# A weighing and a last sum move from VectorE to ScalarE copies and GpSimd operations, and a GpSimd step waits for VectorE's gate

## The reference

```python
h = tok(x)                                   # position, nesting and segment embeddings, times W
h = h + attention(layernorm(h))              # 8 heads of 16, softmax over 512 keys, output matrix
xf = layernorm(h)
g = softmax(xf @ gate_w.T) - sigmoid(xf @ thr_w.T) / 4        # 4 experts
w = max(g, 0);  w = w / (sum(w) or 1)                         # (n, 4)
hidden = relu(einsum('ni,ehi->neh', xf, fc1_w))
lo = einsum('neh,ehr->ner', hidden, lora_A)                   # rank 16
lo = einsum('ner,ero->neo', lo, lora_B)
out = einsum('ne,ned->nd', w, einsum('neo,edo->ned', lo, fc2_w))
return h + out
```

## Time and profile before

| what | value |
|---|---|
| time, median of 3 runs | 1127.43 us (1126.55 to 1129.59) |
| the profiled execution's own time | 1126.86 us |
| span in its profile | 1125.1 us |
| PE busy | 1040.1 us, 92% |
| DVE busy | 948.8 us, 84% |
| ACT busy | 807.0 us, 72% |
| POOL busy | 682.1 us, 61% |
| chain that ended last, by engine | PE 64%, DVE 16%, DMA 6%, ACT 5% |

### The profile page before, as it was taken

One profiled execution on the slowest core, in us unless ns is written; L12 is line 12 of the kernel. 1 busy time (PEld: TensorE's weight loads), 2 busy tenths in 40 slices (PEclk: granted clock), 3 DMA queues, 4 the chain that ended last, 5 costly groups with the idle time before them and its releaser, 6 DMA issues.

```text
span 1125.1 us, 20263 instructions
## 1 busy us (share of the span) xinstructions
PE 1040.1 (92%) x6158; PEld 407.9 (36%) x6158; DVE 948.8 (84%) x2442; ACT 807.0 (72%) x1578; POOL 682.1 (61%) x684
## 2 busy tenths in 40 slices
PE   4368999999999999999999999999999999989865
PEld 2112233333434434343433443434343343333322
DVE  7498899999989989899999999999999998887312
ACT  2217787777877788787877778778787777856731
POOL 1855676677666666677666666667766666621231
PEclk9558999999999999999999999999999999999997
DMA  2553645555554445555555545565555554541111
GB/s 74 148 135 89 137 106 135 129 137 127 137 130 124 126 121 130 142 127 134 126 137 126 126 121 132 130 143 126 137 125 137 128 126 113 121 96 36 55 50 32
DMA packets 93530, 132.43 MB, mean 118 GB/s; under 512 B 18205, under 2 KB 69918, under 8 KB 87398
## 3 DMA queue, kind: packets, MB, share of 16 engines
q1 hardware_dynamic: 91872, 129.54, 47.9%
q10 hardware_dynamic: 1550, 1.59, 0.6%
HBM read 89.20 MB, written 35.01 MB: 110 GB/s over the span
## 4 chain that ended last, share of the span: by engine, by line
PE 64%; DVE 16%; DMA 6%; ACT 5%; issue 2%; POOL 1%; SPq 1%; POOLq 0%; ACTq 0%; DVEq 0%
PE pv L737 17%; PE mix L750 15%; PE sc L724 13%; DVE negmax L1025 9%; PE mix L804 7%; DMA den_dram<-ctx_sb 4%; PE mix L787 3%; DVE bn L1015 2%; ACT probs L592 2%; PE mix L809 2%; DVE h L1050 2%; PE mix L825 2%; DMA den<-den_dram 2%; ACT qk L596 1%; PE mix L769 1%
## 5 line engine op out<-in xcount | busy, mean ns | idle before, releaser
L1025 DVE TENSOR_REDUCE negmax<-mix 128x1 f32<-128x512 f32 x1024 | 649.0, 679 | 56.8 <-PE mix L750 56.2
L592 ACT ACTIVATE probs<-sc 128x512 f32<-128x512 f32 x1024 | 556.3, 600 | 118.2 <-PE sc L724 112.0
L724 PE MATMUL sc<-qstk,kstk 120*128 120x512 bf16 x1024 | 364.2, 382 | 5.6 <-ACT probs L592 4.9
L750 PE MATMUL mix<-kstk,qstk 96*128 96x512 bf16 x1024 | 331.7, 395 | 24.6 <-DMA kstk<-stack_dram 7.3
L737 PE MATMUL pv<-probs,vals 128*32 128x512 f32 x2048 | 244.8, 595 | 0.0
L528 POOL TENSOR_TENSOR ctxh<-ctx_sb,rdenb 128x512 f32<-128x512 f32 x64 | 81.0, 1268 | 245.3 <-DMA rdenb<-rden_dram 244.5
L750 PEld LDWEIGHTS mix<-kstk,qstk 96*128 96x128 bf16 x1024 | 89.4, 98 | 266.5 <-DVE negmax L1025 76.1
L724 PEld LDWEIGHTS sc<-qstk,kstk 120*128 120x128 bf16 x1024 | 100.1, 98 | 107.5 <-ACT probs L592 33.4
L804 PE MATMUL mix<-xn2T,fc1T_sb 128*128 128x512 f32 x256 | 138.2, 622 | 0.7 <-ACT hid L646 0.7
L508 POOL TENSOR_TENSOR qk<-qk,rstdb 128x512 f32<-128x512 f32 x64 | 81.1, 1269 | 57.9 <-DMA rstdb<-rstd_dram 53.4
L737 PEld LDWEIGHTS pv<-probs,vals 128*32 128x32 f32 x2048 | 59.1, 109 | 117.4 <-issue 100.1
(11 more groups left out here) (141 smaller groups left out, 1088.5 us busy)
## 6 DMA issues: line engine op xcount, KB each, us to landing
stack_dram<-pieces SPq DMA_DIRECT2D x192, 128.0 KB
rdenb<-rden_dram SPq DMA_DIRECT2D x64, 256.0 KB
qstk<-stack_dram SPq DMA_DIRECT2D x31, 384.0 KB, 6.6
kstk<-stack_dram SPq DMA_DIRECT2D x31, 384.0 KB, 8.8
rstdb<-rstd_dram SPq DMA_DIRECT2D x32, 256.0 KB, 3.4
wrow<-w_dram SPq DMA_DIRECT2D x32, 256.0 KB
out<-out_sb SPq DMA_DIRECT2D x32, 256.0 KB, 2.6
qstk<-stack_dram SPq DMA_DIRECT2D x31, 256.0 KB, 7.0
```

The source lines that it names most:

```text
L592: act.activation(probs[:, c % 8, i % 2], sc[:, i % RING], ACT.Exp).then_inc(s_exp, 1)
L724: pe.matmul(sc[:, i % RING, :], kstk[0:KROWS, u, h, j * P:(j + 1) * P], qstk[0:KROWS, u, h, :], start=True, stop=True).then_inc(s_score, 1)
L750: pe.matmul(max_bank(m), qstk[0:STK, u, h, j * P:(j + 1) * P], kstk[0:STK, u, h, :], start=True, stop=True).then_inc(s_mxmm, 1)
L1025: dve.tensor_reduce(negmax[:, m // NT, m % NT:m % NT + 1], max_bank(m), AX.X, ALU.max, negate=True).then_inc(s_max, 1)
```

## The change

`weigh` and `finish` leave VectorE's list. ScalarE gets two copies out of the `mix` banks, `low` in slot 4 ahead of `qk` and `out` in slot 7, after which the bank is free; GpSimd then multiplies and adds in place in SBUF: `weigh` behind `norm2`, `finish` behind `third` and ahead of `normalise`. TensorE's next users of the two banks wait for the copies. `normalise` of sequence b gets one more wait: until VectorE has finished the gates of sequence b-1 (both belong to one step), except for the last sequence. On SyncE the store of the output moves behind `rden_in`. `add_attention` waits until `finish` of two sequences before has read its buffer of `h2`.

```diff
 ACT_WORK = [
-    (1, 1, "relu", -3, 3), (4, 0, "qk", 3, 0), (4, 0, "qk", 3, 1), (4, 0, "ctx", -1, 1), (6, 0, "xn2T", -2, 0),
-    (8, 0, "gates", -2, 0), (9, 1, "gate_exp", -2, 0), (9, 1, "relu", -2, 0), (10, 1, "relu", -2, 1),
+    (1, 1, "relu", -3, 3), (4, 0, "low", -3, 0), (4, 0, "qk", 3, 0), (4, 0, "qk", 3, 1), (4, 0, "ctx", -1, 1), (6, 0, "xn2T", -2, 0),
+    (7, 0, "out", -3, 0), (8, 0, "gates", -2, 0), (9, 1, "gate_exp", -2, 0), (9, 1, "relu", -2, 0), (10, 1, "relu", -2, 1),
...
 DVE_WORK = [
-    (3, 1, "add_pos", 4, 0), (3, 1, "stats1", 4, 0), (3, 1, "weigh", -3, 0), (6, 0, "stats1", 4, 1),
-    (6, 1, "moments1", 4, 0), (7, 1, "finish", -3, 0), (7, 1, "invert_den", -1, 0),
+    (3, 1, "add_pos", 4, 0), (3, 1, "stats1", 4, 0), (6, 0, "stats1", 4, 1),
+    (6, 1, "moments1", 4, 0), (7, 1, "invert_den", -1, 0),
...
 POOL_WORK = [
-    ("scale", 3, 0), ("add_bias", 3, 0), ("scale", 3, 1), ("rstd2", -2, 0), ("norm2", -2, 0),
+    ("scale", 3, 0), ("add_bias", 3, 0), ("scale", 3, 1), ("rstd2", -2, 0), ("norm2", -2, 0), ("weigh", -3, 0),
     ("second", 3, 0), ("residual", 3, 0), ("third", 3, 0), ("second", 3, 1), ("rstd1", 4, 0),
-    ("residual", 3, 1), ("third", 3, 1), ("normalise", -1, 0), ("v", 3, 0),
+    ("residual", 3, 1), ("third", 3, 1), ("finish", -3, 0), ("normalise", -1, 0), ("v", 3, 0),
 ]
 SP_WORK = [
-    ("piece", 3, (0, 2)), ("ids", 5, 0), ("out", -3, 0), ("piece", 3, (1, 1)), ("rden_out", -1, 0), ("piece", 3, (1, 2)),
-    ("rden_in", -1, 0), ("rstd_out", 4, 0), ("den_out", 0, 0), ("max_in", 1, 0), ("weights_out", -2, 0),
+    ("piece", 3, (0, 2)), ("ids", 5, 0), ("piece", 3, (1, 1)), ("rden_out", -1, 0), ("piece", 3, (1, 2)),
+    ("rden_in", -1, 0), ("out", -3, 0), ("rstd_out", 4, 0), ("den_out", 0, 0), ("max_in", 1, 0), ("weights_out", -2, 0),
...
             def normalise(b, u):
+                if b < NSEQ - 1:
+                    upto(pool, s_gate, b - 1, 13)
...
+            def weigh(b):
+                upto(pool, s_lowcp, b)
+                upto(pool, s_win, b, 16)
+                pool.tensor_tensor(low[:], low[:], wrow[:], ALU.mult).then_inc(s_low, 1)
+
+            def finish(b):
+                upto(pool, s_outcp, b)
+                pool.tensor_tensor(out_sb[:], out_sb[:], h2[:, b % H2], ALU.add).then_inc(s_out, 1)
...
+            def copy_low(b):
+                upto(act, s_lomm, b)
+                upto(act, s_outmm, b - 1)
+                act.copy(low[:], aux("low", 1)).then_inc(s_lowcp, 1)
+
+            def copy_out(b):
+                upto(act, s_outmm, b)
+                upto(act, s_store, b - 1, 16)
+                act.copy(out_sb[:], aux("out")).then_inc(s_outcp, 1)
...
-                "low": (low_rank, (s_low, 1, 1)),
+                "low": (low_rank, (s_lowcp, 1, 1)),
...
-                "out": (experts_out, (s_out, 1, 1)),
+                "out": (experts_out, (s_outcp, 1, 1)),
...
                 upto(dve, s_hc2, b - H2)
+                upto(dve, s_out, b - H2)
                 dve.tensor_tensor(h2[:, b % H2], aux("project"), hb_sb[:, b % HB], ALU.add).then_inc(s_h2, 1)
...
-            def weigh(b):
-                upto(dve, s_lomm, b)
-                upto(dve, s_win, b, 16)
-                upto(dve, s_outmm, b - 1)
-                dve.tensor_tensor(low[:], aux("low", 1), wrow[:], ALU.mult).then_inc(s_low, 1)
-
-            def finish(b, u):
-                upto(dve, s_outmm, b)
-                upto(dve, s_store, b - 1, 16)
-                dve.tensor_tensor(out_sb[:], aux("out"), h2[:, b % H2], ALU.add).then_inc(s_out, 1)
```

More of the change, by code:

```diff
@@ L289, in tower @@
         s_lomm, s_low = sem("s_lomm"), sem("s_low")
+        s_lowcp = sem("s_lowcp")
+        s_outcp = sem("s_outcp")
         s_outmm, s_out, s_store = sem("s_outmm"), sem("s_out"), sem("s_store")
@@ L541, in _ @@
                 "v": lambda b, u, _: value(b, u),
+                "finish": lambda b, u, _: finish(b),
+                "weigh": lambda b, u, _: weigh(b),
                 "residual": lambda b, u, side: residual(b, side),
@@ L653, in _ @@
                 "wT": lambda b, u, _: copy_wT(b),
+                "low": lambda b, u, _: copy_low(b),
+                "out": lambda b, u, _: copy_out(b),
                 "rT": lambda b, u, _: copy_rT(b),
@@ L1121, in _ @@
                 "gate": lambda b, u, part: (gate_first, gate_second, gate_third, gate_fourth)[part](b),
-                "weigh": lambda b, u, _: weigh(b),
-                "finish": lambda b, u, _: finish(b, u),
             }
```

## The result

The changed kernel takes 1134.16 us, the median of 6 runs (1133.16 to 1136.59), against 1127.38 us of the kernel before in the same session (1125.41 to 1129.59): ratio 1.0064, 95% interval 1.005 to 1.0079. That is slower, by 6.8 us. The forecast was 1127.0 us and "no change"; the time lies in the range of 1121 to 1138, but the likeliest case did not happen. The spans of the two profiled executions are 1132.0 and 1125.1 us.

The account below looks back on a forecast made before the run. It took TensorE's work plus a short VectorE stretch as the bound, a floor of 31.19 us a step. Score product 11 +1.8, gates -4.0, end +1.8 sum to -0.4 on 1127.43: 1127.0 us, range 1121 to 1138.

Parts of the forecast that it names:

- the likeliest case: Whole kernel: all is covered in the middle and the ends nearly cancel, 1124 to 1130.5 us; chance 0.49.
- VectorE's relief: Slots 3 and 7: 43 us leave VectorE but are covered by its waits in the middle; 0, at most 8 us gained.
- The rival in which VectorE's lead loosens the steps: Middle steps: VectorE's lead gains 5 to 8 us, less 0.4, giving 1119 to 1122 us; chance 0.17.
- ScalarE's copy of `low`, score product 11: Slot 4: `qk` 0.84 us later, exponential 8 late, TensorE waits 0.13 us; +1.8 us, between 0 and 3.5.
- The same copy, `den_out` later: Denominators' store issued 0.84 us later, hidden by its 2.8 us queue, so landing unmoved; 0, other bound 21 us.
- the rival's "half to all of 21 us": Denominators' loop passes ScalarE's delay on to the steps, 1137 to 1148 us; chance 0.14.
- The third rival: ScalarE holds TensorE at more than one product, 0.3 us a step, none hidden: +8, 1133 us; chance 0.10.
- The copy of `out`: Slot 7: delays two exponentials and `gates` by 0.49 us, not needed at once; 0, at most 0.1 us a step.
- GpSimd's 81 us and the shared port: `weigh` and `finish` on GpSimd: `finish` ends 0.18 us before `cut_max`, so VectorE is not held; 0, bound 34 us.
- The wait of `normalise`: Near the end of the span: four VectorE gate operations no longer held by GpSimd, -4.0 us; in the middle 0.
- The very end: Last product with weights, `out` and last sum: longer multiplication +0.6, copy, handover and longer addition +1.2; +1.8 us.

Follow-up runs that it names:

- extra_gate: Kernel before with `normalise`'s wait, plus one unused 0.68 us VectorE maximum ahead of `invert_den` in every step: 1120.2 us.
- finish_only: Kernel before with only `finish` moved, with its copy of `out`, the output store behind `rden_in` and `normalise`'s wait: 1123.9 us.
- between: Changed kernel with ScalarE's copy of `low` moved from ahead of both halves of `qk` to between them: 1124.8 us.
- the doses: Kernel before with three, six or twelve small ScalarE copies ahead of `qk`, the twelve also with `normalise`'s wait: 1130.6, 1132.8, 1143.7 us.
- dose12_gate: Kernel before with `normalise`'s wait and twelve small unused ScalarE copies ahead of `qk`, delaying it 1.11 us: 1143.7 us.
- order_only: Kernel before with only the output's store moved behind `rden_in`, without `normalise`'s wait: 1133.2 us.
- after_nowait: Changed kernel without `normalise`'s wait for the gates, all else as changed: 1149.5 us.
- weigh_only: Kernel before with only `weigh` moved to GpSimd behind `norm2`, and ScalarE's copy of `low` ahead of `qk`: 1142.3 us.

## Why the prediction was wrong

*VectorE's relief* (0): right. 44 us left VectorE, its wait before `invert_den` grew by 8.3 us over the middle, and `extra_gate`, `finish_only` and `between` show that it has no price there. The rival in which VectorE's lead loosens the steps fell with it: the shortest step did not get shorter.

*ScalarE's copy of `low`, score product 11* (+1.8): this step failed by its size. It said "TensorE waits 0.13 us, in a stretch without slack". The place, the cause and the chain were right. But what waits is the product's weight load, not the product, and once it waits it is no longer hidden under the product before: score product 11 takes 0.39 us in place of 0.22. So the slack was 0.71 - 0.17 = 0.54 us, and the doses give 0.53. That makes 0.29 to 0.30 us in place of 0.13, and 0.33 was measured over a whole step. The other half of the step was right: it said that in steps which already wait for the denominators this "is hidden behind that wait; in the others it counts". With the landings of the kernel before, a shortest step 0.13 us longer would have cost 1.4 us over the 23 steps, close to the 1.8; 0.33 us costs 4.6.

*The same copy, `den_out` later* (0, other bound 21): this step failed too, in part. It asked whether the store lands later, and it does not: the issue moved by 0.87 us, the landing came 0.18 us earlier. It did not ask about the load behind it. In 8 of 23 steps `den_in` lands later behind the last cast than in any step before, though in the mean it is issued no later, and as these steps are set by `invert_den` this costs the other 4.3 us. It is a fifth of the bound, and far from the rival's "half to all of 21 us", but it is not 0. `between` takes most of it away together with the longer shortest step, and `dose12_gate` brings both without the change's work on GpSimd. So it goes with the delay of ScalarE's queue, as far as one trace of each kernel can tell. By what way is open: the piece store between `den_out` and `den_in` is issued 0.87 us later too, so that it ends nearer to `den_in`, but `between` has it nearly as near (2.77 us ahead of `den_in` in the mean, 2.65 after, 3.68 before) with few late landings, and `order_only`, with held gate operations and no delay, has 6 late ones.

So 4.6 + 4.3 = 8.9 us stand where the forecast had 1.8 + 0. The third rival, 0.3 us a step and none hidden, 1133 us, to which the forecast gave 0.10, came near the time by luck: its 0.3 us was right, but a good part was hidden, and late landings made up for it. The same rule explains the two steps behind the middle (63.54 us before and 63.56 after): both waited for the denominators before (31.69 and 31.85 us, above 31.51), so that the 0.33 us is hidden, and what is left is an earlier landing in the first (31.52 after) and a later one in the second (32.03).

*The copy of `out`* (0): right within what can be told; `finish_only` keeps the shortest step of 31.18.

*GpSimd's 81 us and the shared port* (0, bound 34): right for the middle. `cut_max` and `gate_first` were not held in any of its steps. But the margin was read for the wrong operations: the gates behind them are what GpSimd holds, and `order_only` and `after_nowait` show 10 and 14 us of it with the store's new place and no wait. The wait is what kept the forecast's 0 true.

*The wait of `normalise`* (-4.0): right in kind, and the size matches partly by luck. The four steps behind the middle are 4.0 us shorter, all of it in the last. But only three of the four held operations, 2.9 us, lie in that step; another 1.1 us is between the end of the gates and the next `add_attention` (10.3 us before, 9.2 after), and the forecast had no term for it. The fourth operation's 1.1 us lies behind the last cast. There the changed kernel is 1.1 us ahead at the last `add_attention` but one, and 0.1 at the last landing of the weights; why is open. The wait alone gives 1121.3 us, 6 below the kernel before.

*The very end* (+1.8): +2.15 from the last landing on. The term left out is the 0.35 us by which GpSimd starts later behind that landing than VectorE did. It is no constant: `between` has 0.42 us from the landing to the multiplication, the changed kernel 0.43, but `weigh_only` and `after_nowait` 0.13.

Sum of what was found: 0.1 + 8.9 - 4.0 + 2.0 = 7.0 us, for 6.9 between the spans.

## What to carry to other kernels

A copy on an engine with time to spare is priced by what is queued behind it there, not by its duration: find the first instruction of the pacing engine that waits for that queue, take the slack at its weight load, and pay everything above it in every step that nothing else holds up. Then follow every transfer behind that queue to its own landing, not only to the first one. Here the same copy one entry later in the same list costs next to nothing. And where GpSimd works in SBUF on large tiles, a chain of tiny VectorE operations should be kept apart from it by order or by a wait; otherwise a shift of a landing can move the kernel by as much as the edit that is being tried (5.6 us in `order_only`).

## What the runs showed that was not expected

- A 0.17 us operation of VectorE on 128x16 elements takes up to 1.28 us beside a GpSimd instruction of 1.27, and this up to three times within a few microseconds. The number goes from 0 to 14 operations, 0 to 13.6 us, between kernels that differ by one wait or a place in a queue.
- Small ScalarE copies back to back cost 0.09 us each (0.56 us for six of 128x4, 1.11 for twelve of 128x2), though each shows a duration of 0.19 to 0.21 us: the doses had been planned by the duration of one.
- Behind the last landing of `wrow` GpSimd started after 0.43 us (0.13 in `weigh_only` and `after_nowait`), VectorE after 0.08.
- The load of the denominators, always the same transfer at nearly the same place of the step, took 1.5 to 3.5 us, and the longer steps follow its landing to a few hundredths of a us.
- A store issued 1.2 us later in a busy queue landed at the same time (14.84 and 14.72 us), while one 128 KB store less ahead of it moved the landing by 0.53 us.
